# Graph-attention and pair-product block on one core: the x projections in row halves over bank pairs, pair statistics in two batches

## The chip, the cores and the metric

The kernel runs on one core of a Trainium2 chip. The metric is the device time of one execution in microseconds. The reader meets five engines: TensorE (PE, matmuls and transposes into PSUM), VectorE (DVE), ScalarE (ACT), GpSimd (POOL) and the SyncE queue (SP) that issues most of the DMAs. Each engine works through its own instructions in program order; they wait for each other by semaphores.

## The reference

Everything lives on a grid of 128 x 32 tokens with 64 channels. First comes a block over pairs, then a graph attention with a mixture of four experts. Cut to what matters:

```
zn  = ln(ln_c(x)); pn = ln(protein_pair); cn = ln(compound_pair)     # over 64 channels
ab1 = sigmoid(zn G1) * (zn L1) * mask;  ab2 = sigmoid(zn G2) * (zn L2) * mask
pp  = sigmoid(pn G2) * (pn L2);         cp  = sigmoid(cn G1) * (cn L1)
blk = einsum('bikc,bkjc->bijc', pp, ab1) + einsum('bikc,bjkc->bijc', ab2, cp)
x   = x + sigmoid(zn EG) * (ln(blk) LAS) * mask
h   = ln(x) W_gat                                  # 4096 nodes, 4 heads x 4
for each of 262144 edges (src, dst) and a loop at each node:
    e = leaky_relu(a_src[src] + a_dst[dst]);  softmax over the edges of one dst
    agg[dst] += h[src] * alpha
gate = softmax of the top 2 of 4 scores of ln(agg)
x   = x + sum_e gate_e * (gelu(x W1_e + b1_e) W2_e + b2_e)
```

Edge numbers are drawn up to 16384, while there are 4096 nodes. Sources beyond the last node are clamped to it; edges whose destination is beyond are dropped.

## The kernel before, in words

Each partition holds 32 tokens. The kernel is written engine by engine, with every wait by hand; there is no scheduler, so the order of the lines in an engine's block is the order of the work.

**Edges.** VectorE forms one sort key for each edge (`work`, L1175 to L1180). `compact` (L1065) then takes the largest keys of each of 16 stretches of 128: a round is 16 MAX8 instructions (L1071), and between two rounds come 16 MATCH_REPLACE8 (L1081) that remove what was taken. Three rounds give 24 keys a stretch. `between` is called after each half-round, and `statistics(n)` uses these places for the work of the pair block. A small merge (L1209 to L1219) and some 25 operations (L1224 to L1250) turn the keys into eight digits in bf16 (`feats`) and raise `feats_ready`; SyncE sends them through memory (L405, L407). Then come 64 *shows*: TensorE broadcasts two rows' keys into PSUM bank 4 or 5 (L904) and VectorE takes the eight largest of each (L1345). The loop over shows (`m`) is the frame for the rest of the pair block: the constants `AT_...` name the show after which a step stands. `merge` (L1197) sorts the candidates, and L1386 and L1388 write row indices. GpSimd issues 160 indirect DMAs, one for each slot (L539), the first as soon as 32 indices are there and the node rows are stored. A second `compact` of six rounds works on the clamped edges' keys (`clamped`): its first round stands ahead of the shows, the others beside the gathers.

**Statistics.** `groups` are 11 pieces of tokens: 0 and 1 are x, 2 is compound (half size), 3 to 10 are protein, each of 16 tiles. For each one: `total` (VectorE, L1024), `center` (GpSimd, L487 and L489), `square` (ScalarE, L602), `total_sq` (VectorE, L1029), a square root in a batch (ScalarE, L631), `scale_batch` (VectorE reciprocal, L1119), `divide` (GpSimd, L498). x is scaled twice over, by `x_scale` (L1102). The pair groups are in three batches.

**Projections.** `turn_tiles` (TensorE, L801) transposes a piece, `copy_tile` (ScalarE, L606) brings it back, `project_x`, `project_comp` and `project_protein` (L808 to L836) project it with a bias matmul first; `sigmoid` (ScalarE) and `read_bank` (VectorE, L1087) form the gated product and free the bank. There are 16 x projections (NX) over four banks, 4 compound (NCP) and 16 protein (NPR) over two. `EARLY` says how many projections stand ahead of the shows; the remaining proteins stand one in each show. ScalarE switches its function table between square root and sigmoid.

**GpSimd's order** is written out at L500 to L526: centring, the two products for the clamped keys (L479, L481), divides, `owner_w`, and last the masking of `ab` and `sig`, which TensorE's transposes of `ab` (AT_TURN_AB) need.

**Behind the shows.** Experts run on TensorE and ScalarE beside the gathers. VectorE sorts on, sums `dslot`, builds one-hots (L1480), and scans the gathered rows in three parts (L1485); then follow a second round of 32 gathers (L555), the softmax, the gate and the sum into the output.

## Time and profile before

| | us |
|---|---|
| median of 3 runs | 536.95 (536.87 to 538.07) |
| profiled execution, its own time | 537.98 |
| its span, first to last instruction | 536.1 |
| DVE busy | 395.6 (74%) |
| POOL busy | 271.2 (51%) |
| PE busy | 250.9 (47%) |
| ACT busy | 156.5 (29%) |
| HBM read and written | 15.3 MB, mean 29 GB/s |

A line of the profile names the engine, the line of the kernel, the operation, output and input, and how often. Times in a timeline are microseconds from the start of the span. "idle before" with an arrow is the time that the engine stood still ahead of an instruction, and who ended it. PEclk is the granted clock of TensorE as a share of 2.4 GHz. The engines' busy shares are means over stages that differ, so the rows below go by stage.

### The profile page before, as it was taken

The numbers are of one execution on the slowest core, as the hardware profiler recorded it, in microseconds if no ns is written. First come the engines' busy times: TensorE is split into PE (matmuls) and PEld (weight loads), VectorE is DVE, ScalarE is ACT, GpSimd is POOL, SyncE is SP. The second block draws the span as 40 slices with busy tenths as digits, with TensorE's granted clock in tenths as the row PEclk, the third lists the DMA queues.
The fourth block names the chain that finished last, engine by engine and source line by source line (L and its number), as shares of the span: only waits on it lengthen the run. The fifth ranks groups of instructions, "written<-read, shape, count | busy, mean of one in ns | idle before, by whom it ended". The sixth has DMA issues, their size and how long they took to land.

```text
span 536.1 us, 3949 instructions
## 1 busy us (share of the span) xinstructions
PE 250.9 (47%) x1064; PEld 144.1 (27%) x1064; DVE 395.6 (74%) x961; ACT 156.5 (29%) x308; POOL 271.2 (51%) x271
## 2 busy tenths in 40 slices
PE   0005947568795837780466650074056003991000
PEld 0002314357581506330112110052044002771000
DVE  7999843745759698999999999924940389207997
ACT  2635435225111011360999991000000000001100
POOL 6079775600001000077777777776777716770091
PEclk9999956769796756595586775555555555555555
DMA  9950000010000000011111111111231111110002
GB/s 312 218 108 0 1 0 2 0 59 1 1 1 1 0 0 2 30 10 10 10 11 11 11 9 11 10 11 9 83 37 10 10 40 31 10 10 4 0 0 78
DMA packets 26781, 15.58 MB, mean 29 GB/s; under 512 B 22019, under 2 KB 25094, under 8 KB 26246
## 3 DMA queue, kind: packets, MB, share of 16 engines
q1 hardware_dynamic: 20614, 12.94, 9.2%
q0 software_dynamic: 6144, 2.37, 5.9%
q8 instruction: 9, 0.15, 0.1%
q14 instruction: 14, 0.11, 0.1%
HBM read 11.30 MB, written 4.00 MB: 29 GB/s over the span
## 4 chain that ended last, share of the span: by engine, by line
POOL 32%; DVE 28%; PE 23%; issue 11%; DMA 2%; ACT 2%; SPq 0%; POOLq 0%; DVEq 0%; ACTq 0%
POOL stage_c L539 28%; PE bank L969 6%; DVE stage_c L1345 3%; PE bank L815 3%; PE bank L834 3%; DVE xin L1766 2%; PE bank L801 2%; DVE stage_b L1762 2%; DMA bias_in<-in_biases 2%; DVE stage_a L1480 2%; PE bank L904 1%; PE bank L824 1%; PE bank L872 1%; DVE cand L1071 1%; PE bank L936 1%
## 5 line engine op out<-in xcount | busy, mean ns | idle before, releaser
L539 POOL DMA_INDIRECT stage_c<-node_rows,senti x160 | 154.3, 964 | 115.3 <-DVE senti L1388 65.2
L969 PE MATMUL bank<-stage_a 128*128 128x128 bf16 x256 | 65.2, 436 | 94.9 <-DVE stage_a L1480 94.9
L969 PEld LDWEIGHTS bank<-stage_a 128*128 128x128 bf16 x256 | 45.2, 178 | 114.9 <-DVE stage_a L1480 96.3
L746 ACT ACTIVATE stage_a<-stage_a,rows 128x176 f32<-128x176 bf16 x128 | 44.0, 466 | 18.4 <-DVE stage_a L1414 18.4
L1345 DVE MAX8 stage_c<-bank 128x8 f32<-128x192 f32 x128 | 37.5, 351 | 11.4 <-PE bank L904 11.0
L944 PE MATMUL bank<-xnT,late_w 64*128 64x512 f32 x64 | 24.8, 862 | 41.6 <-ACT hid L726 33.0
L555 POOL DMA_INDIRECT stage_c<-slot_rows,taili x32 | 30.2, 943 | 21.8 <-DMA slot_rows<-stage_c 12.4
L1445 DVE TENSOR_REDUCE dslot<-stage_a 128x176 f32<-128x5632 f32 x4 | 38.8, 9704 | 0.0
L1495 DVE TENSOR_TENSOR stage_c<-stage_c,dslot 128x448 f32<-128x448 f32 (+2 forms) x3 | 2.2, 736 | 47.9 <-DMA stage_c<-node_rows,senti 47.9
L904 PE MATMUL bank<-stage_c,owner_w 128*128 128x192 bf16 x128 | 25.3, 299 | 22.6 <-DVE stage_c L1345 22.4
L1480 DVE TENSOR_TENSOR stage_a<-bank,bdc 128x8192 bf16<-128x8192 bf16 x8 | 34.9, 4418 | 0.1
L755 ACT ACTIVATE stage_c<-stage_c 128x448 f32<-128x448 f32 (+2 forms) x6 | 2.1, 390 | 110.3 <-DVE stage_c L1510 110.3
L801 PE MATMUL bank<-ident,stage_a 128*128 128x128 f32 x84 | 14.7, 310 | 36.4 <-POOL stage_a L498 36.4
L529 POOL CAST bdc<-count_i 128x2048 bf16<-128x2048 int32 x1 | 1.9, 1892 | 57.1 <-PE bank L872 57.1
L498 POOL TENSOR_TENSOR stage_a<-stage_a,stats 128x1024 f32<-128x1024 f32 (+1 forms) x11 | 19.8, 1822 | 11.4 <-DVE stats L1119 11.3
L801 PEld LDWEIGHTS bank<-ident,stage_a 128*128 128x128 f32 x84 | 12.0, 165 | 38.6 <-POOL stage_a L498 36.7
L834 PE MATMUL bank<-scaled_w,tT 128*128 128x128 f32 x128 | 21.8, 322 | 0.0
L1099 DVE TENSOR_TENSOR stage_a<-bank,psig 128x256 f32<-128x256 f32 x16 | 9.3, 593 | 16.6 <-ACT psig L624 16.6
L1081 DVE MATCH_REPLACE8 stage_c<-stats,stage_c 128x128 f32<-128x128 f32 x80 | 21.0, 299 | 0.0
L815 PE MATMUL bank<-scaled_w,tT 128*128 128x384 f32 x32 | 20.9, 748 | 0.0
L904 PEld LDWEIGHTS bank<-stage_c,owner_w 128*128 128x128 bf16 x128 | 11.0, 115 | 34.5 <-DVE stage_c L1345 33.1
L587 POOL TENSOR_TENSOR stage_b<-stage_b,stage_c 128x704 f32<-128x704 f32 x4 | 7.3, 1865 | 25.1 <-DVE stage_c L1755 25.1
(312 smaller groups left out, 629.9 us busy)
## 6 DMA issues: line engine op xcount, KB each, us to landing
stage_a<-in_pp SPq DMA_DIRECT2D x8, 512.0 KB, 7.9
stage_c<-node_rows,senti POOLq DMA_INDIRECT x160, 2.4
stage_c<-in_edges SPq DMA_DIRECT2D x2, 1024.0 KB, 8.7
slot_rows<-stage_c SPq DMA_DIRECT2D x1, 1344.0 KB, 4.8
xin<-in_x SPq DMA_DIRECT2D x1, 1024.0 KB, 5.6
out<-xin SPq DMA_DIRECT2D x2, 352.0 KB, 2.7
stage_c<-slot_rows,taili POOLq DMA_INDIRECT x32, 2.4
slot_rows<-stage_c SPq DMA_DIRECT2D x1, 480.0 KB, 2.5
```

The lines of the kernel that those rows point to most:

```text
L539: g.indirect_dma_start(out=gath[:, l, :], out_offset=None, in_=node_rows[:, :], in_offset=bass.IndirectOffsetOnAxis(ap=locali[:, 2, l:l + ...
L555: g.indirect_dma_start(out=agg_in[:, j, :], out_offset=None, in_=slot_rows[:, :], in_offset=bass.IndirectOffsetOnAxis(ap=taili[:, j:j + 1] ...
L746: ins = a_.activation(segd[:, h % 2, j, :], seg[:, j, :], ACT.Copy, scale=rows[:, j, HF + HEADS + h:HF + HEADS + h + 1])
L801: mm = p_.transpose(bank[n % 2][:, P * m:P * (m + 1)], src, ident[:, :])
L815: p_.matmul(ps[:, 0:6 * E], tT[:, b, m, :], bdz, start=False, stop=True, skip_group_check=True).then_inc(projected, 1)
L834: mm = p_.matmul(ps[:, 2 * E * m:2 * E * (m + 1)], tT[:, b, m, :], bdp, start=False, stop=True, skip_group_check=True)
L904: mm = p_.matmul(ps, owner_w[:, row % RPT, :], keys, start=True, stop=True, skip_group_check=True)
L944: mm = p_.matmul(bank[q][:, :], w1s[E * q:E * (q + 1), e, :], xnT[E * q:E * (q + 1), 4 * b:4 * b + 4, :].rearrange("p t n -> p (t n)"), st ...
L969: mm = p_.matmul(pair_ps, high[:, :, c], low[:, :, c], start=(b == 0 and c == 0), stop=(b == OHB - 1 and c == PAIRS - 1))
L1345: v.max(coll[:, 8 * k:8 * k + 8], bank[4 + m % 2][:, SENT * r:SENT * (r + 1)]) \
L1445: v.tensor_reduce(dslot[:, h], segd[:, h % 2].rearrange("p j l -> p l j"), AX.X, ALU.add) \
L1480: ins = v.tensor_tensor(onehot[:, b % 2, h].rearrange("p k (a c) -> p k a c", c=REP), every_k.to_broadcast([P, 64, OHC // REP, REP]), coun ...
```

## The change

It reorders the first half of the kernel. The edges' keys, the shows and everything behind the gathers keep their instructions.

- `bias_in` is loaded second instead of fifth.
- x first: the squares' sums of groups 0 and 1 and the scaling of x (`x_first`, `x_second`) stand among the key products ahead of the first sweep. GpSimd divides x directly behind `owner_w`. ScalarE loads its square root table at the start.
- Eight x projections in place of 16. Each covers four pairs of tokens: the upper 64 rows of the transposed tile are projected into one bank, the lower 64 into the next, by four matmuls of 192 columns on half of the rows, in place of matmuls of 384 columns on all rows with a block-diagonal weight half of which is zero. ScalarE and VectorE take both banks in one instruction. The banks are now one PSUM tensor, and `places` gives each projection its bank or banks; proteins rotate over four.
- Pair statistics in two batches, compound with four protein groups and four protein groups.
- The merge of the keys follows the sweeps directly, with the second scaling and the compound products inside it, then the features. GpSimd waits for `feats_ready` ahead of divides 7 and 8; two of the masking products stand ahead of divides 9 and 10.
- Eight proteins ahead of the shows instead of ten, eight in shows 1 to 8. All later marks move by two shows.
- The first round on the clamped keys moves from ahead of the shows to the other five, beside the gathers. `dst_ok` gets room of its own.

The core of the diff; the parts left out only adapt counts and waits to the new numbering, and of ScalarE's order and of `statistics` only the new order stands, without the removed lines:

```diff
+    banks = ctx.enter_context(nc.psum_tensor("bank", [P, 8 * 512], F32))
+    bank = [banks[:, 512 * n:512 * (n + 1)] for n in range(8)]
...
-    NX, NCP, NPR, NLAS = NC // 2, NC // 8, P // 8, NC // 8
+    NX, NCP, NPR, NLAS = NC // 4, NC // 8, P // 8, NC // 8
...
+    def places(n):
+        if n < NX:
+            return (2 + 2 * (n % 3), 3 + 2 * (n % 3))
+        if n < NX + NCP:
+            return ((4, 5, 2, 3)[n - NX],)
+        if n < NX + NCP + NPR:
+            return ((6, 7, 2, 3)[(n - NX - NCP) % 4],)
+        return (2 + n % 2,)
+    def reads_before(n):
+        return max((k + 1 for k in range(n) if set(places(k)) & set(places(n))), default=0)
...
-    EARLY = NX + NCP + 10
+        return bank[places(n)[0]]
+    def x_bank(n):
+        a = places(n)[0]
+        return banks[:, 512 * a:512 * (a + 2)].rearrange("p (q s) -> p q s", q=2)[:, :, 0:6 * E] \
+            .rearrange("p q (m f) -> p q m f", m=2)
+    def x_tokens(ap, n):
+        return ap[:, 4 * n:4 * n + 4, :].rearrange("p (m q) f -> p q m f", q=2)
+    EARLY = NX + NCP + 8
+    PROTEINS_FROM = 1
+    def protein_at(m):
+        return 0 <= m - PROTEINS_FROM < NX + NCP + NPR - EARLY
     BLOCK_EVERY = 1
-    AT_TURN_AB, AT_BLOCKS, AT_SUM, AT_CENTER, AT_SUMSQ, AT_SCALE, AT_TURN_NB = 8, 9, 20, 22, 26, 30, 32
-    AT_LAS = (34, 36, 38, 40)
-    AT_UPDATE = (36, 38, 40, 42)
-    AT_TOKENS, AT_TOKEN_SQUARES, AT_TOKEN_SCALE, AT_TURN_XN = 44, (47, 48), 52, 54
-    batches = [(XT, CT + 2 * GT), (XT + CT + 2 * GT, 3 * GT), (XT + CT + 5 * GT, 3 * GT)]
+    AT_TURN_AB, AT_BLOCKS, AT_SUM, AT_CENTER, AT_SUMSQ, AT_SCALE, AT_TURN_NB = 10, 11, 22, 24, 28, 32, 34
+    AT_LAS = (36, 38, 40, 42)
+    AT_UPDATE = (38, 40, 42, 44)
+    AT_TOKENS, AT_TOKEN_SQUARES, AT_TOKEN_SCALE, AT_TURN_XN = 46, (49, 50), 54, 56
+    batches = [(XT, CT + 4 * GT), (XT + CT + 4 * GT, 4 * GT)]
+    LAST_OF = (7, 11)
...
+        sp.dma_start(bias_in[:, :], biases[:, :]).then_inc(bias_landed, 16)
         sp.dma_start(xin[:, :, :], x.rearrange("a i j e -> (a i) j e")).then_inc(x_in, 16)
         sp.dma_start(edst, edges[1].rearrange("(p c) -> p c", p=P)).then_inc(edges_in, 16)
...
-        for n in range(3):
-            center(n)
-        clamped_keys()
-        divide(0)
-        divide(1)
-        for n in range(3, 7):
-            center(n)
-        for n in range(2, 5):
-            divide(n)
-        center(7)
+        center(0)
+        center(1)
         pool.wait_ge(row_weights, 1)
         g.tensor_tensor(owner_w[:, :, :], row_w[:, :].unsqueeze(1).to_broadcast([P, RPT, P]), wide(row_block[:, :], P),
                         ALU.mult).then_inc(owners_ready, 1)
-        center(8)
-        for n in range(5, 8):
+        divide(0)
+        divide(1)
+        clamped_keys()
+        for n in range(2, 11):
+            center(n)
+        for n in range(2, 7):
             divide(n)
-        center(9)
-        center(10)
-        for n in range(8, 11):
-            divide(n)
+        pool.wait_ge(feats_ready, 1)
+        divide(7)
+        divide(8)
...
+        divide(9)
+        divide(10)
...
+        a_.activation(tstd[:, 0:1], eps[:, 0:1], ACT.Sqrt)
         square(0)
         square(1)
         act.wait_ge(edges_in, 32)
         a_.activation(dst_next, edst, ACT.Identity, bias=limits[:, 0:1])
+        act.wait_ge(sumsq, 2)
+        a_.activation(xr[:, 0], tssq[:, 0:XT], ACT.Sqrt, bias=eps[:, 0:1], scale=1.0 / E).then_inc(std_x, 1)
         a_.activation(clamped, esrc, ACT.Sign, bias=limits[:, 1:2]).then_inc(act_, t.up())
+        act.wait_ge(var2_x, 1)
+        a_.activation(xr[:, 3], xr[:, 2], ACT.Sqrt, bias=eps[:, 1:2]).then_inc(std2_x, 1)
         act.wait_ge(act_, t.n)
         a_.activation(clamped, clamped, ACT.Relu)
         a_.activation(dst_ok, edst, ACT.Sign, bias=limits[:, 2:3], scale=-1.0).then_inc(act_, t.up())
         act.wait_ge(act_, t.n)
         a_.activation(dst_ok, dst_ok, ACT.Relu).then_inc(clamped_parts, 1)
+        act.wait_ge(keys_ready, 1)
+        a_.activation(yscratch, work, ACT.Sign, accum_out=counts[:, 0:1]).then_inc(keys_counted, 1)
+        copy_tile(0)
+        copy_tile(1)
+        sigmoid(0)
+        sigmoid(1)
+        copy_tile(2)
+        sigmoid(2)
         act.wait_ge(scratch_free, 1)
         act.wait_ge(keys_counted, 1)
         a_.activation(yscratch, clamped, ACT.Sign, accum_out=counts[:, 3:4]).then_inc(keys_counted, 1)
+        square(2)
         square(3)
+        sigmoid(3)
+        copy_tile(3)
         square(4)
+        sigmoid(4)
+        sigmoid(5)
         square(5)
+        square(6)
+        sigmoid(6)
+        sigmoid(7)
         std_batch(0)
+        for n in range(7, 11):
+            square(n)
+        copy_tile(4)
+        copy_tile(5)
+        std_batch(1)
+        for n in range(NX, NX + NCP):
             sigmoid(n)
+        copy_tile(6)
...
+        def project_x(n, b, i):
+            if reads_before(n):
+                pe.wait_ge(bank_read, reads_before(n))
+            for a in places(n):
+                p_.matmul(v3(bank[a][:, 0:6 * E], 3 * E), ones_row[:, :],
+                          zbias[:, 0:3 * E].unsqueeze(1).to_broadcast([3, 2, 3 * E]), start=True, stop=False,
+                          skip_group_check=True)
+            for m in range(2):
+                for q, a in enumerate(places(n)):
+                    mm = p_.matmul(bank[a][:, 3 * E * m:3 * E * (m + 1)], tT[E * q:E * (q + 1), b, 2 * i + m, :],
+                                   bdz[E * q:E * (q + 1), 3 * E * q:3 * E * (q + 1)], start=False, stop=True,
+                                   skip_group_check=True)
+            mm.then_inc(projected, 1)
...
         def statistics(n):
 
             if n == 0:
                 total(2)
                 total(3)
                 total(4)
+            elif n == 1:
                 total(5)
                 total(6)
+                total(7)
+                for k in range(3):
+                    read_bank(k)
+            elif n == 2:
+                total(8)
+                total(9)
+                total(10)
                 total_sq(2)
                 total_sq(3)
+                for k in range(3, 6):
+                    read_bank(k)
                 total_sq(4)
             elif n == 3:
                 total_sq(5)
                 total_sq(6)
+                read_bank(6)
+                read_bank(7)
+                scale_batch(0)
+                total_sq(7)
+                total_sq(8)
             elif n == 4:
+                total_sq(9)
+                total_sq(10)
...
+        total_sq(0)
+        total_sq(1)
         dve.wait_ge(edges_in, 32)
         v.tensor_scalar(plain_src, esrc, float(LAST), None, ALU.is_lt).then_inc(vec, t.up())
         v.scalar_tensor_tensor(ktmp, edst, float(NODES), esrc, ALU.mult, ALU.add).then_inc(vec, t.up())
-        dve.wait_ge(vec, t.n - 1)
+        x_first()
+        settle()
         v.scalar_tensor_tensor(plain, edst, float(NODES), plain_src, ALU.is_lt, ALU.mult).then_inc(vec, t.up())
+        x_second()
...
-        scale_batch(1)
-        for k in range(8, 12):
-            read_bank(k)
-        total(9)
-        total(10)
-        for n in range(8, 11):
-            total_sq(n)
-        for k in range(12, NX):
-            read_bank(k)
-        scale_batch(2)
-        for k in range(NX, NX + NCP):
-            read_bank(k)
...
+        scale_batch(1)
+        for n in range(NX, NX + NCP):
+            read_bank(n)
...
+        dve.wait_ge(keys_counted, 2)
         for n in range(NX + NCP, EARLY):
             read_bank(n)
-        dve.wait_ge(keys_counted, 2)
-        dve.wait_ge(normed, len(groups))
-        compact(clamped, ccand, CH3, NCH3, TAKE3, rounds=range(1))
...
-        compact(clamped, ccand, CH3, NCH3, TAKE3, between=between_sweeps, rounds=range(1, TAKE3 // 8))
+        dve.wait_ge(normed, len(groups))
+        compact(clamped, ccand, CH3, NCH3, TAKE3, between=between_sweeps)
```

## Rows read from the trace of the kernel before

**Rows 1.** Busy time by stage (stretch, length, engines busy, PEclk, DMA share, GB/s).

```profile
24.00:63.00 39.00, 16.64 (x42) 7.28 (x42) 36.13 (x124) 20.31 (x28) 29.66 (x20) 1.00 0.29 53
...
63.00:97.40 34.40, 23.16 (x72) 10.61 (x72) 15.54 (x39) 15.12 (x26) 24.08 (x15) 0.65 0.00 1
...
110.90:136.40 25.50, 21.06 (x134) 16.48 (x134) 12.92 (x58) 9.81 (x20) 0.00 (x0) 0.89 0.10 31
...
149.06:226.50 77.44, 53.69 (x282) 34.22 (x284) 64.67 (x165) 13.06 (x19) 2.25 (x2) 0.67 0.02 6
```

**Rows 2.** VectorE's groups by line, 23 to 111 us (busy, mean | idle, releaser).

```profile
L1024 DVE TENSOR_REDUCE stats<-stage_a 128x16 f32<-128x1024 f32 (+1 forms) x9 | 10.1, 1147 | 0.0
...
L1029 DVE TENSOR_REDUCE stats<-stage_a 128x16 f32<-128x1024 f32 (+1 forms) x6 | 6.7, 1121 | 0.3 <-ACT stage_a L602 0.3
...
L1029 DVE TENSOR_REDUCE stats<-hid 128x16 f32<-128x1024 f32 x5 | 6.0, 1210 | 6.1 <-ACT hid L602 6.1
...
L1091 DVE TENSOR_TENSOR stage_b<-bank,stage_b 128x128 f32<-128x128 f32 x16 | 4.0, 283 | 3.3 <-ACT stage_b L618 3.3
...
L1095 DVE TENSOR_TENSOR cpk<-bank,psig 32x256 f32<-32x256 f32 x4 | 1.7, 413 | 7.0 <-ACT psig L624 7.0
```

**Rows 3.** GpSimd's groups by line, 24 to 97.4 us.

```profile
L498 POOL TENSOR_TENSOR stage_a<-stage_a,stats 128x1024 f32<-128x1024 f32 (+1 forms) x11 | 19.8, 1822 | 11.4 <-DVE stats L1119 11.3
...
L489 POOL TENSOR_TENSOR stage_a<-stage_a,stats 128x1024 f32<-128x1024 f32 (+1 forms) x9 | 16.2, 1805 | 0.7
...
L479 POOL TENSOR_TENSOR stage_c<-stage_c,stage_b 128x2048 f32<-128x2048 f32 x1 | 4.5, 4505 | 0.0
...
L487 POOL TENSOR_SCALAR stats<-stats 128x16 f32<-128x16 f32 (+1 forms) x9 | 2.3, 250 | 18.5 <-DVE stats L1024 17.9
```

**Rows 4.** Timelines around the first gather (start, duration, engine, line; idle before).

```profile
226.33 0.18 DVE L1388 TENSOR_SCALAR senti<-senti 128x32 int32<-128x32 int32 x1
...
227.43 1.17 POOL L539 DMA_INDIRECT stage_c<-node_rows,senti  x1 [65.25 <-DVE senti L1388]
...
368.67 1.27 DVE L1495 TENSOR_TENSOR stage_c<-stage_c,dslot 128x448 f32<-128x448 f32 x1 [17.42 <-DMA stage_c<-node_rows,senti]
```

**Rows 5.** VectorE's timeline ahead of the gathers.

```profile
12.14 0.41 DVE L1158 TENSOR_TENSOR bias<-bank,bias_in 3x256 f32<-3x256 f32 x1 [1.09 <-DMA bias_in<-in_biases]
...
99.26 3.65 DVE L1210 COPY sent<-cand 128x160 f32<-128x160 f32 x1
...
106.00 0.26 DVE L1224 TENSOR_SCALAR stage_c<-sent 128x192 int32<-128x192 f32 x1
...
110.88 1.01 DVE L1099 TENSOR_TENSOR stage_a<-bank,psig 128x256 f32<-128x256 f32 x2
...
148.51 2.19 DVE L1345 MAX8 stage_c<-bank 128x8 f32<-128x192 f32 x8
```

**Rows 6.** Busy time of single sweeps: MAX8, replace, the clamped one.

```profile
23.83:26.93 3.10, 0.00 (x0) 0.00 (x0) 3.10 (x16) 3.10 (x3) 0.00 (x0) 1.00 1.32 217
...
29.77:33.94 4.17, 0.00 (x0) 0.00 (x0) 4.17 (x34) 1.52 (x2) 3.91 (x3) 1.00 0.86 192
...
129.11:136.40 7.29, 3.56 (x28) 2.92 (x27) 7.29 (x49) 2.20 (x5) 0.00 (x0) 1.00 0.00 0
```

**Rows 7.** TensorE's timeline: bias matmuls of five proteins, the first half-height pair.

```profile
111.61 0.58 PE L831 MATMUL bank<-pbias,ones_row 3*128 3x512 bf16 x1 [10.76 <-DVE stage_a L1099]
...
114.98 0.60 PE L831 MATMUL bank<-pbias,ones_row 3*128 3x512 bf16 x1
...
124.90 0.38 PE L831 MATMUL bank<-pbias,ones_row 3*128 3x512 bf16 x1
...
126.74 0.39 PE L831 MATMUL bank<-pbias,ones_row 3*128 3x512 bf16 x1
...
128.75 0.38 PE L831 MATMUL bank<-pbias,ones_row 3*128 3x512 bf16 x1
...
217.69 2.08 PE L944 MATMUL bank<-xnT,late_w 64*128 64x512 f32 x4
```

102 lines of the change are left out of this document (25 added, 77 removed).

## The prediction

> **What bounds the kernel now.** I read the busy time by stage first [rows 1], then the busy time and waits of VectorE and GpSimd by line [rows 2, 3], then VectorE's timeline. The execution has two halves. From 227.4 us on, GpSimd issues 160 row gathers one behind the other [rows 4]; that stretch and the tail behind it start when VectorE has written the first indices (row of L1388, over at 226.5 us). VectorE has slack inside it: 17.4 us before the first scan [rows 4]. So the second half is a block of 536.1 - 226.5 = 309.6 us that moves with its start, and the question is when L1388 is done.
>
> The first half is VectorE's queue. It is 36.1 of 39.0 us busy from 24 to 63, but only 15.5 of 34.4 from 63 to 97.4 and 12.9 of 25.5 from 110.9 to 136.4 [rows 1]. The reader is to see who it waits for. In 63 to 97.4 it stands behind squares and square roots on ScalarE (6.1 us for one square, L1029), which stand behind GpSimd's centring; then behind four compound projections, 7.0 us of waits and 1.7 of work, 2.2 us each [rows 2]. Then the two copies L1209 and L1210 meet GpSimd's masking: 3.65 us for 160 elements, where a 192-element operation behind it takes 0.26 [rows 5]. From 110.9 it waits for protein projections. These are idle times of the engine that sets the end, so they can be won.
>
> **The change, part by part.** I follow VectorE to four marks: sweeps begin, features ready, first show, end of show 8.
>
> Sweeps begin at 23.83 now [rows 6]. Two sums of squares come ahead of them: VectorE's eleven take 12.7 us with one half-sized, so 1.12 each at their pitch, 2.3 together [rows 2]. The x statistics' five small operations come too; none should take more than the 0.41 of a 32x256 product [rows 2], so 1.0 to 2.0, I take 1.5. The two square roots fall beside the key products; the table load that they need is now taken while ScalarE has nothing. The bias lands earlier: it cost 1.09 us of waiting [rows 5], of which x landing one DMA issue later eats most; I credit 0.4. Sweeps begin at 23.8 + 2.3 + 1.5 - 0.4 = 27.2.
>
> From there to the features, VectorE's own work: three MAX8 sweeps at 3.10 and two replace sweeps at 4.17 are 17.6 [rows 6]. Nine sums are 10.1 busy, some 9.6 at their pitch; nine sums of squares likewise 9.6 [rows 2]. Sixteen x products of 128 columns take 4.0; eight of 256 columns are put by the 0.41 of the 32x256 product, less overlap, at 0.36, together 2.9; four compound products 1.5 [rows 2]. Two reciprocals 0.8. The features from L1209 took 110.88 - 97.4 = 13.5; without the two copies' standing in line (5.6 us down to 0.6) they are 8.5 [rows 5]. Sum 50.5. Added to 27.2: 77.7 with no wait at all.
>
> Which waits stay? GpSimd from 27.2: two divides, the clamped keys (two products like L479, 4.5 each), nine centrings (16.2 for the products, 2.3 for the means, and gaps: 20), five divides (19.8 / 11 = 1.8 each, one of half size): 3.7 + 9.0 + 20 + 8.5 = 41.2, over at 68.4 [rows 3]. The last centring is through at about 60. The sums that need its squares come behind the third MAX8 sweep, which ends at about 65.6, and the first feature copy behind them at 68: everything arrives within a few us, but in time. Between the second replace sweep and the third MAX8 stands one square root with a table load on ScalarE, under 1 us of waiting. The compound projections at 2.2 each can start at about 65 and are through at 74, beside 3.2 us of merging; they leave 0.5 to 1.5. I take 2.3 us for all. **Features ready at 80**, against 110.9.
>
> The x projections are hidden. A pair of 64-row, 512-column matmuls takes 2.08 at the low clock [rows 7]. The new ones have two pairs of 192 columns and two bias matmuls: 1.6 to 3.1 us plus about 0.9, whether the halves run beside each other or not. Eight of them are 20 to 32 us, spread over 31 to 60 us where VectorE takes them in three groups; the cover is VectorE's sweeps, and if it is gone the price is up to 8.
>
> First show. Before: ten proteins and 7.3 us of a clamped sweep [rows 6] between 110.9 and 136.4. The sweep leaves this place. Of the eight proteins, four fit in PSUM ahead (they now rotate over four banks) while VectorE computes features. The other four need TensorE at its pace: 126.74 - 124.90 = 1.84 each at the high clock (2.4 GHz), and 114.98 - 111.61 = 3.37 at the low one (1.2 GHz) [rows 7]. TensorE comes from working on the first four, so I take the high clock: 4 x 1.84 plus 2.6 for the wait on GpSimd's divide 7 and hand-overs. First show at 90.
>
> Shows 0 to 8 carry eight proteins: six at 128.75 - 126.74 = 2.01, two without the turn's four transposes at an estimated 1.6 and one plain show at 0.55 (eight maxima, four shows, in 2.19) make 15.8 [rows 5, 7]. GpSimd has divides 7 and 8, two masking products (1.8 each if they run like a divide, 2.8 at most, as they are strided; I take 5 together) and divides 9 and 10 behind the features: 12.4 us, to 92.4 [rows 3]; protein 10 wants divide 9 at about 96, so they are covered by 4 us. The four diagonal copies (L1263) now fall at about 92, on GpSimd's last masking product; 0 to 4 us, I take 1, since TensorE is two shows ahead. End of show 8 at 106.8. The same place of the order before (two shows ahead of the turn of ab) is the end of show 6: 148.51 + 0.55 = 149.06 [rows 5].
>
> From 149.06 to 226.5 are 77.4 us [rows 1] of the same work; the marks are two shows later in the count, so two fewer bare shows stand at the end: -1.1. L1388 is done at 106.8 + 76.3 = 183.1. The clamped sweep joins the gathers: 7.3 of 17.4 us of slack [rows 4]; ScalarE's weighing then waits a few us for VectorE's sums, before that same scan. Nothing of it reaches the end; if the slack were gone it would cost 7.3.
>
> Span 183.1 + 309.6 = 492.7. The profiled execution took 537.98 for its span of 536.1, 1.03 above the median 536.95. So 492.7 + 1.9 - 1.0 = 493.6, of which I give **493.5**.
>
> **A meeting of two engines that speaks against it.** The copy of 160 elements that lasted 3.65 us while GpSimd multiplied [rows 5] shows one engine standing still for the other. The change puts two such meetings on the path: the last key product L1180 is issued together with divides 0 and 1, and the diagonal copies meet masking and divides. If GpSimd goes first in both, the price is two divides, 3.7, and up to 4: 8 us, of which 1 is in the sum. I let VectorE go first at L1180, since that instruction is next in its own queue while GpSimd has yet to see a semaphore. The Trainium skill, page "SBUF — State Buffer", section "Who interferes with whom", says that whichever of the two issues first takes the shared pair of ports for its whole instruction and the other fully blocks, that copies and VectorE operations with two SBUF inputs are among those that meet it, and that reductions never do. By that rule, the trace agrees for the copy, and divides during the sweeps would be free.
>
> **The rivals.**
> - Given back in pieces: both meetings lost (7 more), the four last early proteins at the low clock (4 x 1.5 = 6 more), waits in the sweeps of 3 instead of 2.3. For it: TensorE's mean clock in these stages was 0.65 to 0.89 [rows 1]. Time 500 to 510.
> - The serial chain stays: ScalarE's queue holds the squares behind the count of clamped keys, which stands behind GpSimd's 9 us. If centring and squares run later than I have them by the 18.9 us that VectorE idled in 63 to 97.4 [rows 1], that comes back: 512. Against it: the sums that wait are three sweeps further on.
> - It doesn't do what it says: the statistics are reordered but features come no earlier than before, as each wait only moves. 530 to 538; the 5.6 us at the copies alone speak against it.
> - Slower: half-height matmuls neither overlap nor let the clock rise, and TensorE stays at 1.2 GHz to 183 us. Sixteen proteins at 1.53 more are 24.5; from 149 on, 53.7 busy at 0.67 become 72, 18 more [rows 1]; x projections, no longer covered, 8 x 2.1 = 17. Together 59 against the 43.5 won: 552. It decides from 43.5 us. Against it: the pair at 217.7 us took 2.08 for two [rows 7], and TensorE's mean granted clock in 110.9 to 136.4, where it worked longest without a gap, was 0.89 [rows 1].
>
> **How the numbers follow.** Forecast 0.80 (487 to 500), pieces 0.11 (500 to 510), serial chain 0.04, not what it says 0.02, slower 0.03. Below, 487: all waits at their lower bounds and a free pair of copies give 6.5. Above, the range goes into the second case, to 507. Comparisons tell apart about 0.3% (1.6 us). Faster 0.94, same 0.02, slower 0.04.
>
> **What would show it.** Right: the first MAX8 on the keys at about 27; L1209 at 68, and L1210 with 0.3 us instead of 3.65; first L1345 at 90; L1388 over at 183; 160 gathers at an unchanged pitch; VectorE's wait before the first scan at about 10 us. Wrong: waits above 3 us between the sweeps for ScalarE's squares; a diagonal copy of over 1 us; protein projections 3.4 us apart; or a vanished wait before the first scan, which would mean that the gather stretch is no longer GpSimd's.

## The result, and the profile after

The changed kernel takes 500.5 us (median of 4 runs, 499.64 to 502.37) against 537.48 for the kernel before beside it (4 runs, 536.87 to 538.07): ratio 0.9357, 95% interval 0.9312 to 0.9401 (the quotient of the two medians, 0.931, lies at its edge). The forecast was 493.5, the range 487 to 507. The profiled execution took 501.24 for a span of 499.4. Of some kernels a few executions come out more than 1.5% above the fastest of the same kernel; the ratios given below leave these slow ones out, the medians do not.

The page of the changed kernel, busy times and shares (the lines that answer to the table of before):

```profile
span 499.4 us, 3990 instructions
...
PE 238.6 (48%) x1096; PEld 142.7 (29%) x1096; DVE 392.1 (79%) x952; ACT 151.8 (30%) x297; POOL 273.2 (55%) x271
```

VectorE is now busy for 79% of a shorter span with nearly the same work (392.1 us, 395.6 before). By stage (stretch, length, engines busy, PEclk, DMA share, GB/s): the sweeps, the features, up to the first show, shows 0 to 8, and on to the first indices.

```profile
31.61:72.35 40.74, 28.62 (x118) 16.58 (x119) 40.27 (x140) 24.19 (x31) 38.82 (x27) 1.00 0.04 12
72.35:83.92 11.57, 11.57 (x64) 7.87 (x63) 10.47 (x40) 5.58 (x11) 0.75 (x1) 1.00 0.00 1
83.92:94.11 10.19, 10.19 (x75) 7.92 (x73) 4.56 (x9) 5.56 (x12) 10.06 (x5) 1.00 0.25 79
94.11:113.90 19.79, 17.66 (x122) 14.12 (x121) 13.82 (x32) 7.29 (x16) 5.69 (x3) 0.91 0.00 1
114.40:189.57 75.17, 51.95 (x276) 33.02 (x278) 62.90 (x158) 12.75 (x19) 2.25 (x2) 0.67 0.02 6
```

In the sweeps VectorE works for 40.27 of 40.74 us; the like stretch of before, which began at 23.83, ran to 97.4 and had 18.9 us of idle time from 63 on [rows 1]. The marks of the prediction, with two later executions beside them (e10 is the changed kernel again, e11 a version described below):

| us from the span's start | before | forecast | changed | e10 | e11 |
|---|---|---|---|---|---|
| first MAX8 on the keys | 23.8 | 27.2 | 31.6 | 30.9 | 28.2 |
| first feature copy | 97.4 | 68 | 72.4 | 71.7 | 68.9 |
| features ready | 110.8 | 80 | 83.9 | 82.7 | 81.7 |
| first show | 136.5 | 90 | 94.1 | 92.3 | 91.3 |
| end of show 8 (before: show 6) | 149.1 | 106.8 | 114.3 | 111.2 | 107.6 |
| first indices written | 226.5 | 183.1 | 189.6 | 187.8 | 183.0 |
| end of the span | 536.1 | 492.7 | 499.4 | 497.4 | 492.5 |

From the indices to the end there are 309.8 us (309.6 before): the block moved as one. What it lost is VectorE's wait ahead of the first scan; answering to [rows 4], VectorE's timeline of the changed kernel:

```profile
331.74 1.27 DVE L1529 TENSOR_TENSOR stage_c<-stage_c,dslot 128x448 f32<-128x448 f32 x1 [10.31 <-DMA stage_c<-node_rows,senti]
```

17.42 us became 10.31: the clamped sweep took its 7 us out of a wait (e12 tests this by itself).

Two places came out worse than forecast. Ahead of the sweeps, VectorE's timeline (start, duration, engine, line) and GpSimd's beside it:

```profile
12.12 0.40 DVE L1197 TENSOR_TENSOR bias<-bank,bias_in 3x256 f32<-3x256 f32 x1
12.56 1.61 DVE L1201 CAST parts<-bias 3x256 bf16<-3x256 f32 x1
14.21 3.71 DVE L1204 TENSOR_TENSOR bias<-bias,parts 3x256 f32<-3x256 f32 x1
17.84 0.27 DVE L1206 TENSOR_SCALAR zbias<-parts,ident 3x256 bf16<-3x256 bf16 x1
18.14 0.28 DVE L1201 CAST parts<-bias 3x256 bf16<-3x256 f32 x1
18.46 0.41 DVE L1204 TENSOR_TENSOR bias<-bias,parts 3x256 f32<-3x256 f32 x1
```
```profile
12.13 1.90 POOL L519 TENSOR_TENSOR stage_a<-xin,stats 128x1024 f32<-128x1024 f32 x1
13.98 3.65 POOL L533 TENSOR_TENSOR owner_w<-row_w,row_block 128x2048 bf16<-128x2048 bf16 x1
29.45 5.74 POOL L528 TENSOR_TENSOR stage_a<-stage_a,stats 128x1024 f32<-128x1024 f32 x2 [11.81 <-DVE stats L1148]
```

The reader is to compare 14.21 with 18.46: the same line L1204, the same three rows of 256 values, 3.71 us the first time and 0.41 the second. The first ends at 17.92, just behind GpSimd's `owner_w` product (L533, 13.98 to 17.63). The cast ahead of it, L1201, ends at 14.17 behind the centring L519, which is over at 14.03: 1.61 against 0.28 at 18.14. In the kernel before, the bias block (from L1158 at 12.14 to the end of the copies at 15.9) lasted 3.7 us, here it takes 20.30 - 12.12 = 8.2: 3.3 more for the subtraction behind `owner_w`, and 1.2 more for the cast behind the centring, which took 0.43 in the kernel before, at 12.58, when that product had almost ended. And in the shows, VectorE's timeline and TensorE's:

```profile
95.83 0.61 DVE L1131 TENSOR_TENSOR stage_a<-bank,psig 128x256 f32<-128x256 f32 x1 [0.58 <-ACT psig L650]
96.28 4.95 DVE L1296 COPY bdc<-cpk 32x256 f32<-32x256 f32 x4
101.26 0.63 DVE L1378 MAX8 stage_c<-bank 128x8 f32<-128x192 f32 x2
```
```profile
97.91 0.38 PE L863 MATMUL bank<-pbias,ones_row 3*128 3x512 bf16 x1
...
101.95 0.48 PE L936 MATMUL bank<-stage_c,owner_w 128*128 128x192 bf16 x2 [2.12 <-DVE stage_c L1378]
102.36 0.60 PE L863 MATMUL bank<-pbias,ones_row 3*128 3x512 bf16 x1
...
105.79 0.39 PE L863 MATMUL bank<-pbias,ones_row 3*128 3x512 bf16 x1
```

The four diagonal copies at 96.28 take 4.95 us, 1.54 in the kernel before, beside GpSimd's last masking product (L553, 96.19 to 99.81), which began 0.09 us ahead of them; e2 tests whether that is the cause. TensorE stands idle for 2.12 us, and the protein behind the gap takes 105.79 - 102.36 = 3.43 in place of 2.01.

### The profile page after: what moved, and what is told of

It reads as the page before. It is cut to its first block, busy times and chain, and to the rows that moved or that the text cites. A ratio compares the mean times of both kernels' runs of the same rounds, so it can differ in the third digit from the quotient of the medians.

```text
span 499.4 us, 3990 instructions
## 1 busy us (share of the span) xinstructions
PE 238.6 (48%) x1096; PEld 142.7 (29%) x1096; DVE 392.1 (79%) x952; ACT 151.8 (30%) x297; POOL 273.2 (55%) x271
## 4 chain that ended last, share of the span: by engine, by line
DVE 34%; POOL 30%; PE 19%; issue 12%; DMA 2%; ACT 1%; POOLq 0%; DVEq 0%; SPq 0%; ACTq 0%
POOL stage_c L566 30%; PE bank L1001 7%; DVE stage_c L1378 4%; PE bank L866 3%; DVE xin L1800 2%; PE bank L828 2%; DVE stage_b L1796 2%; DVE stats L1056 2%; DVE stage_a L1514 2%; DVE xn L1113 2%; DVE stats L1061 1%; PE bank L856 1%; PE bank L936 1%; PE bank L904 1%; DMA xin<-in_x 1%
## 5 line engine op out<-in xcount | busy, mean ns | idle before, releaser
L582 POOL DMA_INDIRECT stage_c<-slot_rows,taili x32 | 30.2, 944 | 21.8 <-DMA slot_rows<-stage_c 12.3
L936 PE MATMUL bank<-stage_c,owner_w 128*128 128x192 bf16 x128 | 25.0, 296 | 19.8 <-DVE stage_c L1378 19.6
L528 POOL TENSOR_TENSOR stage_a<-stage_a,stats 128x1024 f32<-128x1024 f32 (+1 forms) x11 | 21.7, 2002 | 23.1 <-DVE stats L1148 11.8
L1529 DVE TENSOR_TENSOR stage_c<-stage_c,dslot 128x448 f32<-128x448 f32 (+2 forms) x3 | 2.2, 735 | 40.8 <-DMA stage_c<-node_rows,senti 40.8
L828 PE MATMUL bank<-ident,stage_a 128*128 128x128 f32 x84 | 15.8, 324 | 34.2 <-POOL stage_a L528 34.2
L976 PEld LDWEIGHTS bank<-xnT,late_w 64*128 64x128 f32 x64 | 6.4, 246 | 56.7 <-ACT hid L753 42.7
L866 PE MATMUL bank<-scaled_w,tT 128*128 128x128 f32 x128 | 19.4, 297 | 0.0
L1103 DVE MAX8 stats<-stage_c 128x8 f32<-128x128 f32 x96 | 19.2, 292 | 0.0
```

What stands on the lines that cost most here:

```text
L582: g.indirect_dma_start(out=agg_in[:, j, :], out_offset=None, in_=slot_rows[:, :], in_offset=bass.IndirectOffsetOnAxis(ap=taili[:, j:j + 1] ...
L828: mm = p_.transpose(bank[n % 2][:, P * m:P * (m + 1)], src, ident[:, :])
L866: mm = p_.matmul(ps[:, 2 * E * m:2 * E * (m + 1)], tT[:, b, m, :], bdp, start=False, stop=True, skip_group_check=True)
L936: mm = p_.matmul(ps, owner_w[:, row % RPT, :], keys, start=True, stop=True, skip_group_check=True)
L976: mm = p_.matmul(bank[q][:, :], w1s[E * q:E * (q + 1), e, :], xnT[E * q:E * (q + 1), 4 * b:4 * b + 4, :].rearrange("p t n -> p (t n)"), st ...
```

## The experiments

e1 to e4 ran on one chip, and e8 and e10 to e12 on another, each with the kernel before beside them (536.83 and 536.55). In the session of e5, e9, e6 and e7 every kernel, before included (664.22), took over 120 us more. In the four traces of that session the loss lies behind the first gather, 442.5 to 443.6 us from the indices to the end in place of some 309.5, while the stretches ahead of it ran as elsewhere; why is not known. These four are compared with each other and by marks, and e9 and e7 were run again as e11 and e12.

**e1: `owner_w` at a later place**, behind the divides and ahead of the pause:

```diff
         center(1)
-        pool.wait_ge(row_weights, 1)
-        g.tensor_tensor(owner_w[:, :, :], ...).then_inc(owners_ready, 1)
         divide(0)
...
+        pool.wait_ge(row_weights, 1)
+        g.tensor_tensor(owner_w[:, :, :], ...).then_inc(owners_ready, 1)
         pool.wait_ge(feats_ready, 1)
```

> The changed kernel (500.5 us), with GpSimd's product owner_w moved from ahead of the x divides to behind divide 6, where GpSimd otherwise idles. Theory A (the bias operations of VectorE stand still behind this product: 3.71 us for a 3x256 subtraction that takes 0.41 elsewhere): the subtraction is back at 0.41, the first MAX8 on the keys starts 3.3 us earlier (28.3 instead of 31.6), all marks behind it move by the same, time 497.2. Theory B (the stretch is set by ScalarE's and the DMAs' times, and the stall only hides another wait): the first MAX8 stays at 31 to 31.6, time 500.5.

499.82 us (ratio 0.9327, 0.9284 to 0.937). The sweeps begin at 27.10, 4.5 us earlier, of which 1.2 is x that landed at 6.82 instead of 8.03; the other 3.3 are what Theory A had put. L1204 is back at 0.41. But the time stayed at 499.8, where Theory A had 497.2, and VectorE's timeline of e1 at the features says where one part went, with GpSimd's beside it:

```profile
12.99 0.41 DVE L1204 TENSOR_TENSOR bias<-bias,parts 3x256 f32<-3x256 f32 x1
```
```profile
68.65 3.64 DVE L1241 COPY sent<-cand 128x160 f32<-128x160 f32 x1
```
```profile
68.55 3.64 POOL L540 TENSOR_TENSOR owner_w<-row_w,row_block 128x2048 bf16<-128x2048 bf16 x1
```

The product began 0.10 us ahead of the copy of 160 elements, which now takes 3.64 in place of 0.23: the same 3.4 us are paid 54 us later. Features are ready at 82.2 instead of 83.9. From the last protein product in the shows to the indices e1 took 77.2 us against 75.7, and the rest went there. The granted clock does not explain this: it was 0.63 against 0.67, but e10 took 77.0 us at 0.67, so such differences come between executions of one kernel too. The mechanism holds, the place was badly chosen.

**e5: `owner_w` first**, ahead of the centring of x:

```diff
+        pool.wait_ge(row_weights, 1)
+        g.tensor_tensor(owner_w[:, :, :], ...).then_inc(owners_ready, 1)
         center(0)
         center(1)
-        pool.wait_ge(row_weights, 1)
-        g.tensor_tensor(owner_w[:, :, :], ...).then_inc(owners_ready, 1)
```

> The changed kernel with owner_w as GpSimd's first product, ahead of the centring of x, while VectorE waits for x. Moving it behind divide 6 took 4.5 us off the start of the sweeps, and then one feature copy stood 3.64 us behind it there. Theory A (the meeting was the cost, and here it meets nothing): the bias subtraction takes 0.41, no feature copy above 1 us, first MAX8 on the keys at 28 to 29, features ready 3 us earlier than in the changed kernel, time 497.5. Theory B (the centring of x, now up to 1 us later, stands in front of the bias operations instead): first MAX8 at 30.5 or later, time 499.5.

Sweeps at 28.15, features at 79.9, indices at 183.9, against 30.9, 82.7 and 187.8 in e10. L1204 is at 0.41 and no feature copy is above 1 us, but the place is not free of meetings, as Theory A had it. VectorE's timeline of e5 and GpSimd's:

```profile
12.40 0.41 DVE L1204 TENSOR_TENSOR bias<-bias,parts 3x256 f32<-3x256 f32 x1
12.74 1.91 DVE L1206 TENSOR_SCALAR zbias<-parts,ident 3x256 bf16<-3x256 bf16 x1
```
```profile
12.64 1.93 POOL L519 TENSOR_TENSOR stage_a<-xin,stats 128x1024 f32<-128x1024 f32 x1
```

The centring of x is 1.2 us later than in e10 (its second product ends at 14.57 against 13.35), and now L1206, 0.27 us in the changed kernel, stands behind it for 1.6 us. In return the scaling of the weights (L1192) takes 0.94 instead of 1.65, as no centring runs beside it. Counted from the landing of x, the sweeps begin after 23.58 us in the changed kernel and in e10, after 21.23 in e5 and after 20.28 in e1. So the meeting with `owner_w` costs 3.3 us, and the move of e5 wins 2.35 of them, all kept up to the features.

**e2: the diagonal copies between the compound products and the features**, while GpSimd pauses:

```diff
         for n in range(NX, NX + NCP):
             read_bank(n)
+        compound_diagonals()
...
-            if m == 1:
-                compound_diagonals()
```

> The changed kernel, with the four diagonal copies moved from show 1 to directly behind the compound products, where GpSimd pauses. Theory A (the copies meet GpSimd's masking and divides, and TensorE's queue runs dry behind them and loses its high clock): the copies take 1.5 us instead of 4.95, features are ready 1.5 us later, first show to end of show 8 shrinks from 20.2 to about 16 us, TensorE has no 2.1 us gap at show 4; time about 498. Theory B (TensorE sets the pace of these shows anyway and the copies were covered): the 1.5 us are simply added, time 502.

497.71 us (0.9294, 0.9257 to 0.9332). The copies take 1.59 us, and from the first show to the last protein product there are 15.9 us in place of 19.8: Theory A, which had 498. The rival, 1.5 us simply added, fell. But features come later (85.7; x landed at 8.64 here), and TensorE waited 2.54 us ahead of the fifth protein; this one and the next took 3.39 us each, at a granted clock of 0.50, so some of the gain went there. That is not in the edit itself: e11 has the same edit and a wait of 1.97 us at the same place, and its proteins go on 1.84 apart.

**e9 and e11: both edits at once.** e9 is e5 and e2 together; e11 is e9 again, beside e10, the changed kernel again.

> owner_w first and the diagonal copies behind the compound products, together. Theory A (the two meetings are separate costs on one path): 3.3 + 2.8 us under the changed kernel, 494.5, which is what the forecast gave without them. Theory B (TensorE's waits and its clock give part of it back, as its queue runs dry before the features are ready): a gap of over 2 us ahead of the fifth protein projection, next projections 3.4 us apart, time 496 to 498.

> The changed kernel, unaltered, beside the other three. Theory: the median within 0.4% of the changed kernel's 500.5 us; L1204's first subtraction at 3.6 to 3.7 us behind owner_w again, the four diagonal copies at 4 to 5 us again, since both meetings follow from the order of the lines. Rival (the meetings are luck of one execution): one of them at its short duration, 0.4 or 1.6 us, with the end of show 8 earlier by as much.

> The changed kernel with owner_w ahead of the centring of x and the diagonal copies behind the features. Theory A (both meetings were on the path, and each is worth what its owner shows): sweeps begin 3.5 us earlier and show 8 ends 5 to 7 us earlier than in the changed kernel beside it; of that TensorE, which has less cover, gives 1 to 2 back; 494.5 to 496.5 against 500.5. Rival B (TensorE is what is late next): the end of show 8 comes earlier, but the last protein to L1388 takes that much longer, and the time is within 1.5 us of the changed kernel's.

e9 took 629.04 beside e5's 630.59: intervals that overlap (0.9433 to 0.9534 and 0.9458 to 0.9555), and by marks the indices at 183.0 against 183.9. TensorE's wait was 1.88 us, with no protein at the low clock behind it, so the rival's 3.4 us did not come; but the diagonal copies gave 0.9 us where Theory A had 2.8. e10 took 499.61 (0.9339, 0.9294 to 0.9385), and both meetings were there again: 3.71 us for L1204, 5.25 for the copies. They are no accident of one execution. e11 took **495.29** (0.9249, 0.9212 to 0.9287), 4.3 us below e10 and the fastest of all. In its profile the indices are done 4.7 us earlier. Theory A had 494.5 to 496.5, and so it came out, but not by its parts: show 8 ends 3.6 us earlier than in e10, not 5 to 7, and TensorE gave nothing back behind it (75.8 us to the indices against 77.0). The shows of e11, VectorE's timeline, and those of e10 below say why the diagonal copies gave so little:

```profile
75.18 1.60 DVE L1261 COPY bdc<-cpk 32x256 f32<-32x256 f32 x4
...
95.01 0.60 DVE L1131 TENSOR_TENSOR stage_a<-bank,psig 128x256 f32<-128x256 f32 x1 [0.95 <-ACT psig L650]
...
97.02 0.60 DVE L1131 TENSOR_TENSOR stage_a<-bank,psig 128x256 f32<-128x256 f32 x1 [0.96 <-ACT psig L650]
```
```profile
94.47 5.25 DVE L1296 COPY bdc<-cpk 32x256 f32<-32x256 f32 x4
...
102.64 0.60 DVE L1131 TENSOR_TENSOR stage_a<-bank,psig 128x256 f32<-128x256 f32 x1 [0.35 <-ACT psig L650]
```

In these shows of e11 VectorE waits about 0.96 us for a sigmoid that waits for TensorE, one protein in 2.01 us. 5.25 us of copies in that stretch (e10, second fence) cost 18.5 - 15.9 = 2.6 us of it, as part runs in VectorE's waits. Moved ahead of the features, where VectorE never waits, the 1.6 us of copying cost 1.75 (e9's features at 81.63, e5's at 79.88). Net 0.9. A place between shows 5 and 9, when GpSimd is through, might pay neither; it was not tried.

**e4: no pause.**

```diff
-        pool.wait_ge(feats_ready, 1)
         divide(7)
```

> The changed kernel without GpSimd's wait for the features; divides 7 and 8, masking and divides 9 and 10 follow as soon as their statistics allow, at about 77 us, in the middle of the compound products and features. Theory A (each copy or two-input operation of VectorE can stand behind a whole GpSimd product): the 25 feature operations, 4.9 us alone, grow by 5 to 9 us; the diagonal copies, in return, no longer meet GpSimd and win back 3 to 4; time 502 to 506. Theory B (the pause buys nothing): features unchanged at 84, diagonal copies free, time 497.

511.55 us (0.9546, 0.9509 to 0.9584): 11.7 above e1 beside it, and 11.0 above the changed kernel's 500.5. VectorE's and GpSimd's timelines of e4 in the features:

```profile
77.48 0.60 DVE L1258 TENSOR_SCALAR stage_c<-sent 128x192 int32<-128x192 f32 x1
...
78.32 1.64 DVE L1261 TENSOR_SCALAR stage_c<-stage_c 128x192 int32<-128x192 int32 x1
79.88 4.79 DVE L1263 TENSOR_SCALAR stage_c<-stage_c 128x192 int32<-128x192 int32 x2
84.58 1.95 DVE L1265 TENSOR_SCALAR stage_c<-stage_c 128x192 int32<-128x192 int32 x1
86.45 5.54 DVE L1265 TENSOR_SCALAR dslot<-stage_c 128x192 int32<-128x192 int32 x2
92.03 0.43 DVE L1268 TENSOR_SCALAR cand<-stage_c 128x192 f32<-128x192 int32 x2
```
```profile
76.06 3.78 POOL L528 TENSOR_TENSOR stage_a<-stage_a,stats 128x1024 f32<-128x1024 f32 x2 [4.01 <-DVE stats L1153]
79.80 2.87 POOL L547 TENSOR_TENSOR stage_b<-stage_b,early_w 128x1024 f32<-128x1024 f32 x1
82.62 1.92 POOL L549 TENSOR_TENSOR stage_b<-stage_b,early_w 128x1024 f32<-128x1024 f32 x1
84.51 3.78 POOL L528 TENSOR_TENSOR stage_a<-stage_a,stats 128x1024 f32<-128x1024 f32 x2
88.25 3.63 POOL L552 TENSOR_TENSOR stage_b<-stage_b,early_w 128x2048 f32<-128x2048 f32 x1
```

An operation of 192 integers takes 0.25 us alone (0.43 for two at 92.03). Here seven of them fill the time from 77.48 to 92, each ending with one of GpSimd's seven products, which follow each other without a gap. The features take 95.23 - 71.29 = 23.9 us in place of 11.6, 12.3 more where Theory A had 5 to 9, so the time lies above its 502 to 506; the rival, features unchanged, fell. The diagonal copies, in turn, find GpSimd idle and take 1.57.

**e8: the pause alone, in the kernel before.**

```diff
+        pool.wait_ge(feats_ready, 1)
         pool.wait_ge(bank_read, NX)
         pool.wait_ge(early_in, 16)
```

> The kernel before with one added wait: GpSimd waits for the features ahead of the masking of ab and sig. Theory A (the two copies L1209 and L1210 stand behind the masking products; without them each takes what its size takes): the copies take 0.6 us in place of 5.6, the features are ready at 106 in place of 110.9, and as the masking is wanted only at show 8 nothing is later for it: about 532 against 537, ratio 0.991. Rival B (the masking of ab, now 10 us later, is late for TensorE's transposes of ab, or meets other VectorE operations in the shows): L1388 ends within 1 us of where it ended, ratio 0.999 to 1.001.

531.92 us against 536.55 (12 and 17 runs; 0.993, 0.9893 to 0.9967). By the ratio that is 3.8 us, with 1.8 to 5.7 in its interval: Theory A, and not the rival's 0.999 to 1.001. VectorE's timeline, answering to the 3.65 of [rows 5]:

```profile
101.03 0.25 DVE L1210 COPY dslot<-cand 128x224 f32<-128x224 f32 x1
101.21 0.22 DVE L1211 COPY sent<-cand 128x160 f32<-128x160 f32 x1
```

The copies take 0.25 and 0.22, and the features 8.3 us, where the prediction had put 8.5. This profiled execution reached the copies 3.7 us later than the one of before (101.03 against 97.36), for a reason taken up in the last section, and still wrote the indices 2.4 us earlier (224.1 against 226.5).

**e6: x late.** GpSimd forms the clamped keys ahead of the divides of x:

```diff
+        clamped_keys()
         divide(0)
         divide(1)
-        clamped_keys()
```

> The changed kernel with GpSimd's two products for the clamped keys ahead of the divides of x, as in the kernel before; nothing else moved. Theory A (the early x divides carry the gain: the x projections must run beside the first two sweeps): x is divided some 13 us later, VectorE waits 7 to 9 us ahead of the first three x products, time 508. Theory B (the squares and centring of the pair groups set the pace of the sweeps' stretch, x only has to be there at its end): waits under 2 us, time 501.

From the first MAX8 to the first feature copy 49.4 us in place of 40.7; VectorE's timeline has the waits:

```profile
47.57 0.42 DVE L1123 TENSOR_TENSOR stage_b<-bank,stage_b 128x256 f32<-128x256 f32 x1 [3.57 <-ACT stage_b L645]
49.90 0.42 DVE L1123 TENSOR_TENSOR stage_b<-bank,stage_b 128x256 f32<-128x256 f32 x1 [1.91 <-ACT stage_b L645]
53.27 0.42 DVE L1123 TENSOR_TENSOR stage_b<-bank,stage_b 128x256 f32<-128x256 f32 x1 [2.95 <-ACT stage_b L645]
```

They sum to 8.4 us, inside Theory A's 7 to 9, each for ScalarE's sigmoid of an x projection, though each x product itself takes 0.42. 9 us of GpSimd ahead of x reach VectorE almost whole: x first is a necessary part of the gain. The indices came at 194.9, 7 us behind e10's; the time, 642.03, is that of the disturbed session.

**e3: full rows.** Two 384-column matmuls on all rows, one for each bank, in place of the four half-height ones, with the tokens assigned to the banks accordingly:

```diff
-        return ap[:, 4 * n:4 * n + 4, :].rearrange("p (m q) f -> p q m f", q=2)
+        return ap[:, 4 * n:4 * n + 4, :].rearrange("p (q m) f -> p q m f", q=2)
...
-            for m in range(2):
-                for q, a in enumerate(places(n)):
-                    mm = p_.matmul(bank[a][:, 3 * E * m:3 * E * (m + 1)], tT[E * q:E * (q + 1), b, 2 * i + m, :], ...)
+            for q, a in enumerate(places(n)):
+                mm = p_.matmul(bank[a][:, 0:6 * E], tT[:, b, 2 * i + q, :], bdz, start=False, stop=True, ...)
```

> The changed kernel with the x projections as matmuls on all 128 rows with 384 columns (the block-diagonal weight) again, still two banks a projection. Theory A (the x projections are hidden under the sweeps, as forecast): time 500.5 within 1 us. Theory B (TensorE is at its low clock throughout this stretch, 1.65 us for one such matmul, so a projection grows by 1.65 us and VectorE waits for the sigmoids of x between its sweeps): waits of 4 to 8 us in all ahead of the x products, time 505 to 508.

502.34 us (0.9376, 0.9329 to 0.9424), 2.5 above e1 with an overlapping interval; sweeps to copies 41.93 against 40.74, with waits of 0.45 and 0.41 us that the changed kernel has not. That is between the two theories and nearer to A. TensorE's timelines of one projection in the changed kernel and in e3:

```profile
36.03 1.65 PE L845 MATMUL bank<-scaled_w,tT 64*128 64x192 f32 x8
```
```profile
35.94 2.93 PE L844 MATMUL bank<-scaled_w,tT 128*128 128x384 f32 x4
```

The row halves save 1.3 us in each such projection (four of e3's eight took 1.56 instead of 2.93, at a faster pace that the last section takes up), and 1 to 2 us of the time, which is within the noise of these runs; the rest of TensorE's time is hidden either way.

**e7 and e12: the clamped sweep moved, alone, in the kernel before.**

```diff
-        compact(clamped, ccand, CH3, NCH3, TAKE3, rounds=range(1))
...
-        compact(clamped, ccand, CH3, NCH3, TAKE3, between=between_sweeps, rounds=range(1, TAKE3 // 8))
+        compact(clamped, ccand, CH3, NCH3, TAKE3, between=between_sweeps)
```

> The kernel before, with one part of the change alone: the first round on the clamped keys moves from ahead of the shows to the other five, beside the gathers. Theory A (it is 7.3 us on the path there and covered here): show 0 follows the last early protein at 129, time 529.5, or down to 527 if TensorE, which then has no 4.5 us gap, keeps its high clock in the shows; VectorE's wait before the first scan falls from 17.4 to about 10 us. Theory B (the gathers' stretch has no real slack, ScalarE's weighing and VectorE's sums get later and with them the first scan): 537.

> The kernel before with the clamped keys' first sweep beside the gathers, and nothing else. Theory A (the stretch behind the first gather has room for it, 17.4 us of waiting ahead of the first scan): L1388 ends 6.5 to 7 us earlier, VectorE's wait ahead of the first scan shrinks by about 7, and the time is 530 against 537, ratio 0.987. Rival B (the gather stretch does not take it for nothing): L1388 as early, but the span behind the first gather longer than 309.6 us by 3 or more; ratio 0.993 or above.

e7: indices at 220.06, 6.5 us earlier, and the time 659.85 against 664.22 (12 and 17 runs; 0.9952, 0.9915 to 0.9989), by the ratio 3.2 us. e12: 528.69 against 536.55 (4 and 17 runs; 0.9865, 0.9799 to 0.9931), by the ratio 7.2 us with 3.7 to 10.8 in its interval. The indices of e12 come 12 us earlier, but 3.6 of these stand ahead of the features and are not the sweep's; from features to indices e12 took 107.3 us and e7 108.5, against 115.7 in the kernel before and 114.7 in e8. The interval of e12 alone doesn't exclude the rival; the trace does: 309.5 us from the indices to the end, and the wait ahead of the first scan (answering to [rows 4]) is

```profile
356.64 1.27 DVE L1494 TENSOR_TENSOR stage_c<-stage_c,dslot 128x448 f32<-128x448 f32 x1 [10.37 <-DMA stage_c<-node_rows,senti]
```

## Why the prediction was right, and which terms were off

- **What bounds the kernel**: right. The second half is a block that moves with its start. From the indices to the end there are 309.3 to 309.8 us in every trace outside the one session named above, whatever the front did. In that session it was some 443, and there too the same to 1.1 us.
- **Sweeps begin at 27.2**: measured 31.6, the largest miss. The two sums took 2.26 (2.3), the x statistics 1.2 (1.5), the wait for the bias is gone whole (1.2 where 0.4 was credited). What failed is that the bias block was costed at nothing; the term for it is 4.5 us. Of these 3.3 are the meeting with `owner_w`, which now stands behind the centring of x, beside the bias operations; e1 shows it. The other 1.2 are the cast behind the centring itself: the bias operations, which no longer wait for their data, begin while that product runs, and so the cast takes back what the earlier bias had won. x landing at 8.03 instead of 6.87 adds 1.2. In the ten traces with x in this order it landed anywhere from 6.8 to 8.6 (median 7.1), in the four with the old order from 6.7 to 6.9, so most of that is chance, and a few tenths may belong to the change. The prediction held the rule and named two meetings, and did not list the bias operations among them.
- **The meeting at L1223** (L1180 before): right. VectorE went first, 2.29 us, and GpSimd's two divides took 5.74 instead of 3.76, off the path.
- **Sweeps to features 52.8**: measured 52.3. Waits of VectorE in it are 0.2 (squares), 0.2 (x products) and 0.7 for the compound, 1.1 where 2.3 was taken, while its own work took 51.2 where 50.5 was summed: two small misses that partly cancel. 40.8 was forecast for the stretch up to the first copy, and it took 40.74, so close by luck too. The rival of the serial chain, 512, fell here: VectorE never waited more than 0.2 us for squares. e6 shows what would have made it wait: x, not the squares.
- **The pause**: the copy of 160 elements takes 0.23 us. The sum credited 5.0 us for the copies; e8 gives 3.8 for the kernel before, with 5.0 inside its interval. In the changed kernel the pause is worth 11, as without it divides 7 to 10 and all masking fall into the features (e4).
- **x projections hidden**: right, with 1 to 2 us owed to the row halves (e3). The four half-height matmuls took 1.65 us, the lower end of 1.6 to 3.1: the halves ran beside each other.
- **First show**: 10.2 us behind the features, forecast 10; four proteins at the high clock, 1.84 apart.
- **Shows 0 to 8**: 20.2 measured, 16.8 forecast. Without their meeting the stretch takes 16.3 (e11: 15.9 and 0.4 for the last maxima), where 15.8 was summed; the term of the diagonal copies was 1 and is 3.9: 2.6 as in e10, and some 1.4 for the one protein at the low clock (granted 0.56 from 101.9 to 105.8) behind the gap that they made. The argument that TensorE is two shows ahead covered only a part, because TensorE waits for VectorE's maxima to free its banks (row of 101.95). Copies of over 1 us each and proteins 3.4 us apart were two of the signs that the prediction had named for being wrong; both were seen, at this one place.
- **To the indices**: 75.3 measured, 76.3 forecast.
- **The clamped sweep in the gathers**: right, 7 us off that wait and 10.3 us of it left (e12 and the trace).

The sum of the misses in the spans: 4.4 - 0.5 + 0.2 + 3.4 - 1.0 + 0.2 = 6.7, from 492.7 to 499.4. The two large ones are, but for the landing of x, meetings of VectorE and GpSimd. That is the first part of the rival "given back in pieces" (500 to 510), which stood at 0.11, with the bias operations in the place of L1180; its second part, the early proteins at the low clock, did not come. The time lies where the two cases touch, and the mechanism of the miss is the rival's. With both meetings moved, e11 measures 495.3, its span 492.5 where 492.7 was worked out. That this agrees to 0.2 us is partly luck: the marks of e11 lie 0.8 to 1.7 us behind the forecast up to show 8, and the stretch to the indices, 75.4 where 76.3 was put, takes most of that back. The other rivals fell. "Slower" needed TensorE at 1.2 GHz all the way; from the features to the first show proteins came 1.84 apart, and PEclk was 0.91 in shows 0 to 8.

Where the 37 us come from, by one part alone: about 7 the clamped sweep (e7, e12), 3.8 the pause in the old order (e8). Some 26 remain for the new order; undoing x first there gives back 8.7 of them (e6), and undoing the pause 11 (e4), more than it brought in the old order. No run separates the rest: the two batches, the early merge, the banks of the proteins and eight early proteins instead of ten were not undone one by one.

## What to carry to other kernels

Write down, for each product that is moved on GpSimd, every VectorE operation that can stand beside it, small ones too: the price of a copy, a cast, a scalar operation or one with two inputs in SBUF is there the rest of the product, not its own size. Put such products beside sweeps and sums, and short chains of copies and scalar operations where GpSimd pauses; e1 and e5 show that a product moved without such a look takes its meeting along. And a stretch in which the engine has waits can take small work below its price (here 5.25 us of copies for 2.6), so move work out of the stretch that has no waits, not out of the one that has.
